# A graph transformer layer on one core: the output part of the linear attention is divided over both edge attentions, with a residual sum made beforehand

## The reference, cut to what is computed

```
xn = layernorm(x)                       # x: 3125 x 512 (25 tiles of 128 nodes)
g  = xn
for l in range(2):                      # two graph layers over 53125 edges, sorted by dst
    q, k, v = g@Wq[l].T (scaled), g@Wk[l].T, g@Wv[l].T           # 8 heads of 64
    w   = softmax over the edges of a node of q[dst]·k[src]
    agg = segment_sum(w * v[src], dst)
    g   = batchnorm(g + agg@Wo[l].T + bo); g = batchnorm(g + relu(g@W1)@W2)
q, k, v = softmax(xn@Mq.T), softmax(xn@Mk.T), xn@Mv.T            # linear attention
mix = (q @ (k.T v) * D_inv + q) @ Mp.T + bp
x2  = x + layernorm(g)*ln_g + ln_b + mix
out = x2 + mixture_of_experts(layernorm(x2))                     # 8 experts, top 2
```

## Time and profile before

| | |
|---|---|
| median of 3 runs | 3053.66 us |
| the profiled execution | 3058.51 us, its span 3057.2 us |
| PE, DVE, ACT, POOL busy | 87%, 53%, 43%, 36% of the span |
| mean granted clock of PE | 0.939 of full speed |
| head until the first product of qkv | 0 to 41 us |
| qkv 0 and the linear attention's projections | 41 to 496 us |
| attention 0 (its first keys turned at 517) | 516 to 1296 us |
| join 0, finish 0, qkv 1 | 1296 to 1727 us |
| attention 1 (its first q turned at 1738) | 1738 to 2412 us |
| join 1, finish 1 | 2412 to 2619 us |
| mixture of experts | 2619 to 3057 us |

### The profile page before, as it was taken

One profiled execution on the slowest core, in us unless ns is written; L12 is line 12 of the kernel. 1 busy time (PEld: TensorE's weight loads), 2 busy tenths in 40 slices (PEclk: granted clock), 3 DMA queues, 4 the chain that ended last, 5 costly groups with the idle time before them and its releaser, 6 DMA issues.

```text
span 3057.2 us, 78338 instructions
## 1 busy us (share of the span) xinstructions
PE 2651.4 (87%) x32605; PEld 2147.2 (70%) x32605; DVE 1622.6 (53%) x3262; ACT 1324.3 (43%) x3700; POOL 1110.0 (36%) x1130
## 2 busy tenths in 40 slices
PE   5999997989999999849899788888888589589998
PEld 4877885777777777638488677777777466477776
DVE  5236775555555555556612445555555656656543
ACT  3324443555555555422332255555655323334332
POOL 0000002666666666400001267777777212122110
PEclk8999998999999999979899899999999889699898
DMA  5643003889899899641024389999999531122211
GB/s 197 230 178 108 29 28 145 302 312 321 314 322 322 315 317 330 230 135 50 14 97 155 146 325 350 344 353 353 354 353 349 173 110 62 38 88 96 69 60 59
DMA packets 231795, 621.75 MB, mean 203 GB/s; under 512 B 39008, under 2 KB 45792, under 8 KB 231427
## 3 DMA queue, kind: packets, MB, share of 16 engines
q0 software_dynamic: 137088, 466.78, 42.7%
q1 hardware_dynamic: 94339, 149.78, 14.6%
HBM read 538.80 MB, written 103.39 MB: 210 GB/s over the span
## 4 chain that ended last, share of the span: by engine, by line
PE 59%; DMA 15%; POOL 10%; DVE 7%; issue 7%; ACT 2%; SPq 0%; DVEq 0%; POOLq 0%; ACTq 0%
PE ps L1179 5%; PE ps L574 5%; PE ps L575 5%; PE ps L576 5%; POOL Y L1096 4%; DMA Y<-KVd,srcE 4%; PE ps L1222 4%; PE ps L1209 3%; PE ps L774 3%; DMA aggd<-stage,segs 3%; PE ps L942 2%; PE ps L944 2%; PE ps L943 2%; PE ps L1186 2%; POOL WA L1096 2%
## 5 line engine op out<-in xcount | busy, mean ns | idle before, releaser
L1096 POOL DMA_INDIRECT Y<-KVd,srcE x449 | 429.3, 956 | 226.5 <-issue 121.0
L1370 ACT ACTIVATE stage<-ps,stage 128x128 f32<-128x128 f32 x832 | 294.1, 366 | 112.9 <-PE ps L1186 110.0
L1351 ACT ACTIVATE work<-ps 128x512 f32<-128x512 f32 x309 | 179.6, 596 | 303.2 <-PE ps L1179 302.9
L1096 POOL DMA_INDIRECT WA<-KVd,srcE x186 | 178.3, 959 | 360.0 <-PE ps L576 265.6
L1179 PE MATMUL ps<-ident,Y 128*128 128x128 f32 x1796 | 252.7, 280 | 32.3 <-DMA Y<-KVd,srcE 25.5
L1351 ACT ACTIVATE G<-ps 128x512 f32<-128x512 f32 x315 | 181.6, 596 | 224.4 <-PE ps L1179 223.6
L1277 DVE COPY G<-ps 128x512 f32<-128x512 f32 x208 | 143.7, 691 | 238.9 <-PE ps L1186 236.3
L574 PE MATMUL ps<-Wh,xs 128*128 128x512 f32 x600 | 238.5, 397 | 30.5 <-DVE xs L514 30.5
L1179 PEld LDWEIGHTS ps<-ident,Y 128*128 128x128 f32 x1796 | 199.5, 143 | 70.8 <-issue 43.5
L575 PE MATMUL ps<-Wl,xs 128*128 128x512 f32 x600 | 236.6, 394 | 0.0
L576 PE MATMUL ps<-Wh,xs 128*128 128x512 f32 x600 | 236.6, 394 | 0.0
(11 more groups left out here) (383 smaller groups left out, 6772.1 us busy)
## 6 DMA issues: line engine op xcount, KB each, us to landing
KVd<-stage SPq DMA_DIRECT2D x96, 256.0 KB, 2.0
aggd<-work SPq DMA_DIRECT2D x6, 2048.0 KB, 7.4
Qd<-stage SPq DMA_DIRECT2D x48, 256.0 KB, 2.0
G<-aggd SPq DMA_DIRECT2D x48, 256.0 KB, 2.9
Y<-KVd,srcE POOLq DMA_INDIRECT x449
Y<-in_x SPq DMA_DIRECT2D x4, 1536.0 KB, 15.0
G<-mixq SPq DMA_DIRECT2D x24, 256.0 KB
mixd<-rowsb SPq DMA_DIRECT2D x24, 256.0 KB
```

The source lines that it names most:

```text
L1096: pool.indirect_dma_start(out=kvs[a], out_offset=None, in_=KVd[l][:, :], in_offset=bass.IndirectOffsetOnAxis(ap=srcE[:, n:n + 1], axis=0)) ...
L1351: act.activation(kT[n % len(kT)], banks(l)[place_of(l, "k", n) % len(banks(l))][:, :], ACT.Copy).then_inc(out_a, 1)
L1370: last = act.activation(pT[g % len(pT)][:, P * i:P * (i + 1)], SC[g % 2][:, P * i:P * (i + 1)], ACT.Exp, bias=smin[:, t:t + 1], scale=-1.0 ...
```

## The change

- Side work: `SIDE = (range(0, 13), range(13, NT))`. Node tiles 0 to 12 are made in attention 0, 13 to 24 in attention 1; each step has a second, empty `yield`, so that a tile takes eight groups. Attention 1 gets the buffers of attention 0: 20 instead of 25, 3 banks instead of 5, 6 slots for turned keys instead of 7.
- Ready residual: `residual_pool` makes x + (mbp + ln_b) tile by tile on POOL early in the kernel and stores it to `xbd`; the side work loads it (`fetch_xb`) and adds it in place of the bias, and the experts' stage loads one tensor `resd`, four tiles ahead, and has no POOL additions.
- Head: six tiles of x, then the weights in three whole loads into a buffer of their own, between the groups of x; `HEAD = 6`; the first products wait only for their own matrix; the query weights are cut during qkv.
- Joins: the flag is loaded once, before attention 0; `setup_*` stands ahead of `crowded`; piece b is multiplied into banks 0 to b only, 40 products instead of 64.

```diff
-KVN = (20, 25)
+KVN = (20, 20)
+SIDE = (range(0, 13), range(13, NT))
@@ residual_pool, new
+            for t in range(NT):
+                i, r = t % 2, ROWS[t]
+                if t + 1 < NT:
+                    load(t + 1)
+                pool.wait_ge(xb_in[i], 16 * (t // 2 + 2))
+                pool.tensor_tensor(xb_ring[i][0:r, :], xb_ring[i][0:r, :], xb_row[0:r, :], ALU.add).then_inc(xb_made, 1)
+                pool.wait_ge(xb_made, t + 2)
+                pool.dma_start(xbd[P * t:P * t + r, :], xb_ring[i][0:r, :]).then_inc(xb_st, 16)
@@ first_loads
+            six_tiles(0)
+            raw_weights(1)
+            six_tiles(1)
+            raw_weights(2)
+            six_tiles(2)
+            six_tiles(3)
+            raw_weights(0)
@@ head
-        HEAD = 12
+        HEAD, LATER, INDEX_AT = 6, 5, 12
@@ qkv_pe
-            pe.wait_ge(w_lo, (12, 40)[l])
+                if l == 1 and u == 0:
+                    pe.wait_ge(w_lo, 40)
+                if l == 0 and u == NT:
+                    pe.wait_ge(w_lo, 12)
+                    if l == 0 and u == 0:
+                        pe.wait_ge(w_lo, 4 * w)
@@ edge_views, banks
+                kvs = [mt[:, 512:1536], pair(rowsb, 2)] + spare[0:4] + kvs + [pair(G, i) for i in (0, 2)]
+                kT += [G[:, 12 + i, :] for i in range(3)]
-        TURN_BANKS, SC, AG = [[PS[4], PS[2], PS[3]], PS[0:5]], [PS[5], PS[6]], PS[7]
+        TURN_BANKS, SC, AG = [[PS[4], PS[2], PS[3]]] * 2, [PS[5], PS[6]], PS[7]
@@ out_pe (out_sp, out_dve and out_act alike)
-            for s in range(OUT * NT):
-                t, k = divmod(s, OUT)
+            for t, k in itertools.product(SIDE[l], range(OUT)):
...
-                    pe.wait_ge(mq_in, 16 * (t + 1))
+                    pe.wait_ge(mq_in, 32 * (t + 1))
...
                 yield
+                yield
@@ attend_pool
-            early = (6, 9)[l]
+            early = 6
@@ crowded, join
-            for e in (pe, dve, act, pool, sp):
-                e.wait_ge(flag_made, 1)
-            any_ = nc.values_load(flag[0:1, 0:1], min_val=0, max_val=1)
-                for q in range(TB):
+                for q in range(b + 1):
@@ front_pool, removed
-                pool.tensor_tensor(stage[0:r, u, :], stage[0:r, u, :], stage[0:r, 2 + u, :], ALU.add).then_inc(res_mix, 1)
-                pool.tensor_tensor(stage[0:r, u, :], stage[0:r, u, :], rowsb[0:r, 2, :], ALU.add).then_inc(res_row, 1)
@@ attention 1
-        attend_pe(1, iter(()))
+        attend_pe(1, sides[1])
```

More of the change, by code:

```diff
@@ L166, in build @@
         Y0 = tensor("Y0", [P, 12800])
+        with ExitStack() as under:
+            Wraw0 = under.enter_context(nc.sbuf_tensor("Wraw0", [P, 3, 4, 512], F32))
         Wl0 = tensor("Wl0", [P, 3, 4, 512], F32R)
@@ L217, in first_loads, with six_tiles @@
         def first_loads():
-            for g in range(4):
+            def six_tiles(g):
                 sp.dma_start(Yt0[:, 6 * g:6 * g + 6, :],
@@ L290, in columns_act, with high_weight @@
                            ).then_inc(xt_made, 1)
[L292 to L295, removed]
+        def high_weight(n):
+            w, k = CUTS[n]
+            act.wait_ge(w_in[w], 16)
+            act.activation(Wh0[:, w, k, :], Wraw0[:, w, k, :], ACT.Copy).then_inc(w_hi, 1)
         def columns_pe(t):
@@ L606, in build @@
         first_loads()
[L607 to L611, removed]
+        residual_pool()
+        spread_act(0)
+        for n in range(4):
+            high_weight(n)
+        for t in range(2):
+            columns_act(t)
+        for n in range(4, 8):
+            high_weight(n)
+        for t in range(2, HEAD):
+            columns_act(t)
         pe.wait_ge(const_made, 2)
@@ L614, in build @@
             columns_pe(t)
-        for g in range(2):
-            norm_x_dve(g)
-        low_weights()
+        norm_x_dve(0)
+        for n in range(8):
+            low_weight(n)
         index_of_pe, index_of_act, index_of_dve = index_pe(), index_act(), index_dve()
@@ L777, in out_pe, with out_dve @@
                 yield
-        def out_dve(views):
+                yield
+        def out_dve(views, l):
             qT, oT, qb, ob, outb, Wp = views
             yield
-            dve.wait_ge(row_in, 16 * 5)
-            for s in range(OUT * NT):
-                t, k = divmod(s, OUT)
+            for t, k in itertools.product(SIDE[l], range(OUT)):
                 r = ROWS[t]
@@ L2028, in build @@
         views = out_views(G)
-        sides = out_sp(views), out_pe(views), out_dve(views), out_act(views)
+        sides = out_sp(views, 0), out_pe(views, 0), out_dve(views, 0), out_act(views, 0)
         for side in sides:
             next(side)
+        for e in (pe, dve, act, pool, sp):
+            e.wait_ge(flag_made, 1)
+        any_crowd = nc.values_load(flag[0:1, 0:1], min_val=0, max_val=1)
         attend_pool(0, begin0)
@@ L2114, in work_free1 @@
             e.wait_ge(w2_mm, WO)
+        views = out_views(G)
+        sides = out_sp(views, 1), out_pe(views, 1), out_dve(views, 1), out_act(views, 1)
+        for side in sides:
+            next(side)
         attend_pool(1, begin1)
-        attend_pe(1, iter(()))
-        attend_dve(1, iter(()), begin1, work_free1)
-        attend_act(1, iter(()), begin1, work_free1)
+        attend_pe(1, sides[1])
+        attend_dve(1, sides[2], begin1, work_free1)
+        attend_act(1, sides[3], begin1, work_free1)
+        for side in sides:
+            for _ in side:
+                pass
         ends_sp(1)
+        out_done(sp, 1)
         layer_weights(1)
@@ L2238, in front_sp @@
             for s in range(STEPS):
[L2239 to L2240 removed]
+                if 8 <= s < 8 + len(tiles) and tiles[s - 8] + 4 < NT:
+                    fetch_res(tiles[s - 8] + 4)
                 if s == 23:
@@ L2490, in moe_sp @@
             sp.wait_ge(m_st, 16 * NT)
-            fetch_res(0)
-            fetch_res(1)
+            for t in range(4):
+                fetch_res(t)
             sp.dma_start(wg, A["Wg"].rearrange("(k p) e -> p k e", p=P)).then_inc(vec_in, 16)
```

192 lines of the change are left out of this document (104 added, 88 removed).

## The result

The changed kernel takes 3077.7 us (median of 4 runs, 3068.7 to 3082.7) where the kernel before, beside it on the same chip, takes 3052.9: a ratio of 1.0075, 95% interval 1.0054 to 1.0096. It is slower; 3005 was forecast. Its profiled execution took 3068.7 us with a span of 3067.4, which is the low end of its runs, so the two traces differ by 10.2 us and the medians by 25.

A forecast was written before the change was run, and what follows sets the result against it. Attention 0 was taken as bound by PE with a buffer-release loop, attention 1 by POOL's gathers. Head -12.5, division -10, edges +5, joins -14, experts -17 summed to -48.5: median forecast 3005 us, range 2953 to 3045.

The forecast's parts named there:

- Division of the side work: Both attentions: side tiles spread over eight groups make every group 6.90 us, 1435 against 1445 us in all, -10 us.
- T: Time of one group of four edge tiles in the attentions, claimed as (L + W)/2 plus 0.09; 6.90 us taken.
- L: Attentions: time from a buffer's release to the landed tile that refills it, taken as 7.25 us.
- W: Attentions: PE's own work from a turn to the next release, in the heavier of two groups; mean 6.50 us afterwards.
- The bytes: Attention 1: 2.34 MB a group at 351 GB/s needs 6.65 us, under 6.90, so a floor and no term.
- Attention 0 gains, attention 1 gives back: Equal group times in both attentions: attention 0 gains 66 us, attention 1 gives back 55 us.
- Head: Before the first qkv: first product starts at about 25 us instead of 41.04; -12.5 us, bounds -8 and -16.
- Edges: Starts of the attentions: PE waits longer at the first group, with fewer tiles fetched ahead; +5 us.
- Joins: After each attention: setup moved beside the barrier, flag loaded early, fewer selection products; -14 us.
- Experts: Last stage: DVE's waits for the residual sum vanish; -17 us, bounds -6 and -25.
- Slower, by the release loop: Rival, attention 1: waiting for released buffers outweighs the savings above T = 7.13; 3078 us at 7.25; chance 0.07.

The follow-up runs named there:

- run 2: The undivided with 20 instead of 25 key-value buffers in attention 1, still 5 banks and 7 key slots: 3060.1 us, ratio 1.0026.
- run 11: The changed kernel with each projection product of the side work done twice (output wrong): 3129.5 us, ratio 1.0236.
- buffers_20_banks_3: The undivided with 20 buffers, 3 turn banks and 6 turned-key slots in attention 1, no side work there: 3057.9 us, ratio 1.0005.
- run 12: The changed kernel with DVE's step 4 of a side tile (reciprocal, quotient, sum) issued at step 5: 3048.0 us, ratio 0.9978.
- the undivided: The changed kernel with all side tiles in attention 0 and attention 1's former 25 buffers, 5 banks and 7 key slots: 3031.5 us, ratio 0.9904.
- run 7: The undivided with the side work's residual tile load cut to 8 of 512 columns (output wrong): 3007.1 us, ratio 0.9849.
- run 13: The kernel of run 12 with key-value buffers released ahead of a group's first two turned tiles: 3020.4 us, ratio 0.9891.
- run 4: The undivided with 20 buffers, 3 turn banks and 6 turned-key slots in attention 1, the same run as buffers_20_banks_3: 3057.9 us, ratio 1.0005.

## Why the prediction was wrong, step by step

**Division of the side work** is the step that failed: "T = (7.25 + 6.50)/2 + 0.09 = 6.96 ... I take 6.90". Measured were 7.31 and 7.25. 0.38 us over 208 groups is 79 us; by the stage table the attentions gave +64.8 where -5 was forecast, which alone turns the sign. The form of the step, one landing and one group's work for two groups, is supported by runs 2 and 11: T rose with fewer buffers while PE then waited for gathers, and more work on PE lengthened a group by about half of itself. Its terms were mis-sized:
- L. I took 7.7 from the readings of 7.35 and 8.19, reduced it by half a turned tile to 7.25, and trusted that because it fitted attention 0 as it was. The chain after reads 7.68 and 8.21 in the mean, and by T = (L + 5.5)/2 + 0.09, buffers_20_banks_3 with its 6.67 needs L = 7.66.
- W. I took 5.25 for a group without side work, by subtraction, where the earlier trace rows read 5.42 directly; runs read 5.43 to 5.50. The mean of the heavier groups was also added up wrong: by the places that gave 3 x 0.96 before, the fourth pair holds one projection step, 5.25 + 0.96 = 6.21 and not 5.84, so the mean is 6.59 and T 0.05 higher, about 10 us.
- The form itself is not exact. With 6.7 for 6.50 and 7.7 for 7.25 it gives 7.29, which is what was measured; but the same 7.7 with the old W of 7.63 gives (7.7 + 7.63)/2 + 0.09 = 7.76 for attention 0 before, where 7.53 was measured. The fit to 7.29 is thus no proof of the two sizes, and the wait of the next item is in the measured 7.3 as well.
- A wait that the formula did not have: PE's for a bank behind DVE's step 4, because I moved the steps by their number in a tile and not by the parity of the group in which they land. Taken away by itself it gave 30 us (run 12).
- "The bytes ... a floor and no term" was wrong. The Trainium skill, "DMA: Bandwidth & Descriptors", section "Where 436 GB/s comes from", gives some 358 GB/s for one core from HBM; read as a floor it says that 321 GB/s at a share of 0.91 leaves room. No window of an attention passed 351 here, which agrees with the figure; the head's 390, over 4 us, lies above it. The runs show that bytes count well below either: two side loads were worth 24 us in the changed kernel, one of them 24 in the undivided (18 and 17 by the ratios), there in part by later landings and in part with a lower clock (run 7).

These effects overlap (57 for 50 + 30 in run 13), and how the 79 us divide among them is open.

**Attention 0 gains, attention 1 gives back**: right in kind. -20.9 for -66, +85.7 for +55. Of the second, 21 to 25 us are the 20 buffers (runs 2 and 4) and 62 the side work.

**Head**, -12.5: measured -12.9. That it is met so closely is luck: the stage ended between 499.7 and 509.0 us in the fifteen kernels with this head, 8 to 17 us ahead of the one trace before. The first product starts at 24.07 us (25 was forecast), behind the value weights and their cut:

```profile
2.37 14.98 DMA Wraw<-in_WvT
17.38 2.19 ACT Wh L340 x4
...
24.07 0.80 PE ps L625
```

**Edges**, +5: from the landing of the last q store to the first turned q tile it was 10.8 us before (1727.00 to 1737.77) and is 10.5 (1688.96 to 1699.50). Nothing is lost there.

**Joins**, -14: stages with a join in them gave -4.3 and -3.6. From the last aggregate to the first selection product join 0 takes 35.0 us for 32.5, so moving the setup and the flag brought nothing; the chain still has an "issue" of 5.93 us there, and now the setup ahead of it and not beside it. From the last aggregate to the first selection product join 1 takes 30.2 us for 29.2: SP's issuing (4.9 us) and the load of W2T into WA (7.51 us) now stand on the chain there; why was not tested. The selection itself fell from 17.5 to 12.7 us and from 17.1 to 13.2: the triangle is worth 4 to 5 each, not 3.

**Experts**, -17: measured -33.9, twice the term and beyond its bound of -25. In every kernel with the ready residual the stage is 398 to 405 us. Waits of PE in it after:

```profile
PE ps L2337 <- DVE Y L2491: 12.5, 1, 12.5
...
PE ps L2650 <- DVE mtR L2705: 2.8, 2, 1.9
```

These were 22.9 and 18.2: 25.8 us. The second went almost whole, where I had taken 11 of the 15 us of DVE's waits. What makes the remaining 8 was not tested.

**The rivals.** "Slower, by the release loop", at 0.07, named the place and the price: it gave 3078 for T = 7.25. That the number is met is partly luck: the savings outside came out 11 us larger than forecast, the profiled execution lies 9 under its median, and DVE's step, which the rival did not name, is in it. It deserved more: the later of two readings of L led to it, and the mean of all 30 in the kernel before, 7.75, stands above the 7.25 taken.

## What to carry to other kernels

When a duration read off the chain and a duration fitted to a total disagree, the form of the sum is in doubt too: read the duration thirty times and not twice, and give the case that goes by the reading a weight of its own. When an edit moves an instruction to test a wait, look also whether the engine's own busy time changed, and measure the dose of an added piece of work in the trace before judging by it. Where work is spread by a step counter over groups that alternate, look where each step lands in the alternation, on every engine and not only on the bound one: a copy that frees a bank behind 2.2 us of other work stops PE. Where gathers in flight are limited by buffers, a load beside them can cost below the highest rate too; moving it to a stage with idle queues gave 21 us here (3031.5 to 3010.1), twice what the division was forecast to bring.

## What was not expected of the hardware

One load of 0.26 MB every four groups (2.7% of the bytes), at a DMA share of 0.89 and 318 GB/s, cost 23 of 799 us in attention 0, more than its 19.5 us at the 351 GB/s of attention 1, and more than half of it showed as PE's own busy time at a mean clock of 0.97 for 0.99. And twenty or twenty-five buffers for the same gathers are 25 us apart where PE is busy for only 5.5 of 6.4 us and POOL's 6.3 was thought to be the bound.
